# First attention: the transposes of the last chunk's heads stand before the values of the first half, not after them

## What is computed

```python
h = layer_norm(x, ln1_g, ln1_b)
qkv = (h @ w_qkv.T).reshape(B, S, 3, H, hd)      # 16 heads of 16
attn = sliding_window_attn(q, k, v, WINDOW, scale)   # chunks of 128, keys of this and the last chunk
x = x + attn @ w_o.T
```

## Time and profile before

| what | us |
|---|---|
| three runs | 1789.31, 1791.54, 1791.67 |
| median of the runs | 1791.54 |
| span of the profiled execution | 1791.1 |
| PE busy in the span | 1731.2 (97%) |
| first attention, s = 1 to 30 | about 29 to 354 us of the span |

### The profile page before, as it was taken

One profiled execution on the slowest core, in us unless ns is written; L12 is line 12 of the kernel. 1 busy time (PEld: TensorE's weight loads), 2 busy tenths in 40 slices (PEclk: granted clock), 3 DMA queues, 4 the chain that ended last, 5 costly groups with the idle time before them and its releaser, 6 DMA issues.

```text
span 1791.1 us, 43798 instructions
## 1 busy us (share of the span) xinstructions
PE 1731.2 (97%) x15424; PEld 1496.0 (84%) x15424; DVE 1494.1 (83%) x3797; ACT 1197.5 (67%) x3088; POOL 1080.0 (60%) x1060
## 2 busy tenths in 40 slices
PE   6999999999999999999999999989999999999997
PEld 4778777789998888888887888878888888888886
DVE  6888988868878898888987678789898898967776
ACT  6999988854445787877876334358787877743332
POOL 3676556534434778778773455377878777634343
PEclk9999999999999999999999999999999999999999
DMA  3111211032322111111112434331111111131221
GB/s 107 38 37 38 67 44 31 26 107 75 108 63 99 48 41 54 44 52 51 44 43 71 147 105 126 100 103 41 52 44 55 41 54 47 31 102 56 82 82 36
DMA packets 139812, 116.03 MB, mean 65 GB/s; under 512 B 10584, under 2 KB 138848, under 8 KB 138848
## 3 DMA queue, kind: packets, MB, share of 16 engines
q1 hardware_dynamic: 139616, 113.53, 20.5%
HBM read 75.74 MB, written 37.75 MB: 63 GB/s over the span
## 4 chain that ended last, share of the span: by engine, by line
PE 84%; DVE 9%; ACT 3%; issue 3%; POOL 0%; DMA 0%; SPq 0%; DVEq 0%; POOLq 0%; ACTq 0%
PE psum L567 17%; PE psum L569 17%; PE psum L568 17%; PE psum L906 6%; PE psum L874 5%; PE psum L887 5%; PE psum L682 3%; PE psum L664 3%; PE psum L848 3%; ACT a_probs L1718 2%; PE psum L920 2%; PE psum L617 1%; DVE a_neg_max L1211 1%; DVE psum L1209 1%; PE psum L654 1%
## 5 line engine op out<-in xcount | busy, mean ns | idle before, releaser
L1837 ACT ACTIVATE b_probs<-masked,neg_max 128x256 f32<-128x256 f32 (+1 forms) x512 | 250.6, 494 | 124.3 <-DVE neg_max L1343 124.3
L1343 DVE CUSTOM_DVE_ANT_0 masked<-psum,mask 128x256 f32<-128x256 f32 (+1 forms) x512 | 177.3, 412 | 75.9 <-PE psum L874 75.9
L567 PE MATMUL psum<-wa_hi,b_h_hi 128*128 128x512 f32 (+1 forms) x576 | 233.8, 406 | 6.9 <-DVE wa_lo L1138 3.9
L568 PE MATMUL psum<-wa_lo,b_h_hi 128*128 128x512 f32 (+1 forms) x576 | 214.0, 372 | 0.0
L569 PE MATMUL psum<-wa_hi,b_h_lo 128*128 128x512 f32 (+1 forms) x576 | 214.0, 372 | 0.0
L567 PE MATMUL psum<-g_h_hi,wm_hi 128*128 128x512 f32 (+1 forms) x480 | 190.5, 397 | 2.7 <-POOL g_h_lo L2121 1.6
L2070 POOL TENSOR_TENSOR g_in<-g_in,minus_half 128x16 f32<-128x16 f32 x64 | 188.2, 2940 | 4.5 <-DVE g_in L1295 4.5
L568 PE MATMUL psum<-g_h_lo,wm_hi 128*128 128x512 f32 (+1 forms) x480 | 189.3, 394 | 0.0
L569 PE MATMUL psum<-g_h_hi,wm_lo 128*128 128x512 f32 (+1 forms) x480 | 189.2, 394 | 0.0
L1458 POOL TENSOR_TENSOR g_in<-g_z,g_in 128x512 f32<-128x512 f32 x62 | 79.8, 1287 | 143.4 <-DVE g_in L1289 138.2
L567 PE MATMUL psum<-wm_hi,u_hi 128*128 128x256 f32 x576 | 164.3, 285 | 0.1
(11 more groups left out here) (169 smaller groups left out, 5644.0 us busy)
## 6 DMA issues: line engine op xcount, KB each, us to landing
x_mid<-y_out SPq DMA_DIRECT2D x96, 128.0 KB, 1.7
rope_in<-in_rope SPq DMA_DIRECT2D x64, 128.0 KB, 2.2
x_res<-x_state SPq DMA_DIRECT2D x64, 128.0 KB, 2.2
g_in<-x_mid SPq DMA_DIRECT2D x32, 256.0 KB, 3.8
g_old<-x_state SPq DMA_DIRECT2D x16, 512.0 KB, 4.0
out_x<-g_fin SPq DMA_DIRECT2D x15, 512.0 KB, 2.9
w_raw<-in_w_mlp_b SPq DMA_DIRECT2D x2, 2154.0 KB, 8.8
x_in<-in_x SPq DMA_DIRECT2D x32, 128.0 KB, 2.2
```

The source lines that it names most:

```text
L567: nc.tensor.matmul(out, a_hi, b_hi, start=first, stop=False)
L568: nc.tensor.matmul(out, a_hi, b_lo, start=False, stop=False)
L1343: ins = nc.vector.tensor_tensor_reduce(out[:, at], src[:, at], (mask if now else mask0)[:, at], -1.0, BIG, ALU.add, ALU.min, neg_max[:, r, ...
L1837: ins = nc.scalar.activation(out, src, ACT.Exp, bias=neg_max[:, r, k:k + 1], scale=-1.0, accum_out=row_sum[:, n % 2, 4 * r + k:4 * r + k + 1])
```

## The change

In `pe_attention_a`, `transpose_heads(s - 1)` is issued before `values(s, 0)` instead of after it. The waits inside both functions are unchanged, and travel with them. Step 0 has no last chunk, and in step 31 the transposes are issued elsewhere, so steps 1 to 30 differ.

```diff
                 if a_chunk(s):
                     transpose_probs(4 * s + 2)
-                    values(s, 0)
                 if a_chunk(s - 1) and s < NCH - 1:
                     transpose_heads(s - 1)
+                if a_chunk(s):
+                    values(s, 0)
```

## The result

The changed kernel takes 1815.41 us (median of 4 runs, 1812.95 to 1817.37) against 1791.61 us before (median of 4, 1789.31 to 1791.92). The ratio is 1.0133, with a 95% interval of 1.0118 to 1.0147: 1.3% slower, 23.8 us by the medians. The forecast was 1814.5 us, the range 1808 to 1820.

What follows compares the result with a forecast made beforehand. The first attention was taken as a ring of hand-overs among nearly full PE, ACT and DVE, with hardly any reserve. 28 x 0.77 + 2 x 0.70 = 23.0 us on the median 1791.54 gave 1814.5 us, range 1808 to 1820.

Steps and rivals of the forecast that it cites:

- The new wait, 0.77 us a step: Heads' transposes, now first, wait for DVE's q copy (`qt_ready`): 0.72 us plus 0.05 hand-over in each regular step.
- The hand-over from DVE: Time from the end of DVE's q copy to PE's heads load: taken as 0.05 us, up to 0.20 for the range.
- Behind the wait, 1.60 us in either order: On PE, heads 0.59 plus values 1.01 us take the same total, so next scores start 0.77 us later.
- The ring argument: Scores, exponentials, q, L1195, heads, values, scores form a closed ring without slack; the period goes from 10.8 to about 11.6 us.
- the rival of absorption: PE's 0.72 us idle before the probability transposes swallows the new wait: 1793.0 us, chance 0.03; half absorbed near 1803, 0.05.
- The odd steps, 0.70 each: The step opening the second batch and the one at 342.29: differences of 0.65 us, so each costs 0.70 instead of 0.77.
- The sum, 23.0 us: Whole first attention stage: 28 x 0.77 + 2 x 0.70 us, all arriving at the kernel's end.
- the earlier division of the heads: DVE divides heads while PE works on values; gain costed at nothing, as scores leave masking only 0.02 us to gain.
- The faster rival: Division of the heads leaves the chain of waits, taking 0.71 us a step off: 1770.2 us, chance 0.02.
- The clock: Rival: new PE idles lower the granted clock; a quarter of each step low loses 28 us, 1842 us; chance 0.05.
- The weight loads: Heads' first load could be pulled across the wait, saving 0.1 us a step, near 1811.5 us; not used in the sum.
- The signs: Expected in the profile: L693 idle some 0.8 us, L1195 11.5 to 11.6 us apart, ACT's idle before copies up about 0.8.

Runs made afterwards that it cites:

- the run with the wait alone: Old order, with only a wait for `qt_ready` added in front of the first half's values in the same 30 steps, against the kernel before: 1813.87 us, ratio 1.0126.
- The kernel with the heads after three quarters: Heads' transposes issued before the last 8 of the values' 32 matmuls, against the kernel before: 1795.72 us, ratio 1.0026.
- two transposes less: Old order with two of the four heads' transposes left out in chunks 0 to 29, against the kernel before: 1791.44 us, ratio 1.0000.
- the half split: Heads' transposes issued in the middle of the values, 16 of 32 matmuls in front, against the kernel before: 1802.44 us, ratio 1.0061.
- the last kernel: New order with ACT rounding q before exponentials 4s+2 and DVE's `finish_q_t` moved up, against the kernel before: 1808.39 us, ratio 1.0094.

## Why the prediction was right

*The new wait, 0.77 us a step.* Measured: a period of 11.58 against 10.80, 0.78. The hand-over from DVE was taken at 0.05 from another place of the trace and is 0.07 here (224.07 to 224.14). (The prediction counted two more waits behind the released one at that place. For the first chunk the code has one, as for the heads, so the row fitted better than was said.) The idle time in front of the heads is 0.96 or 0.97 us in 29 of the 30 steps and 1.01 in the first. It ends 0.07 us behind the end of L1196 (0.12 in the first), and the run with the wait alone shows that it is the cause.

*Behind the wait, 1.60 us in either order.* 0.59 + 1.01 again.

*Nothing absorbs it.* The 0.72 us in front of the probability transposes are unchanged. The ring argument (every link hangs on the late scores) was right, and from it the rival of absorption falls.

*The odd steps, 0.70 each.* The step at 342.29 before was 342.29 to 353.17, 10.88 us, and is 363.04 to 374.62, 11.58 us: 0.70 as forecast. The one that opens the second batch went from 10.71 us (201.33 to 212.04) to 11.05 us (212.27 to 223.32), only 0.34. There the old order already paid for a part of the delay, in two places:

```profile
201.63 1.19 ACT L1718 ACTIVATE a_probs<-psum,a_neg_max 128x128 f32<-128x128 f32 x4
...
202.15 0.42 PEld L693 LDWEIGHTS psum<-ident,rope_in 128*128 128x128 f32 x4 [0.32 <-issue]
...
202.93 0.22 PEld L654 LDWEIGHTS psum<-k_t_high,q_t 32*128 32x128 f32 x4 [0.36 <-DVE k_t_low L1184]
```

With half of the values the cover was too short. The copy of q ended at 202.08 and the heads loaded 0.07 us later, after 0.32 us idle instead of 0.20: this is the wait of the new order, small, in the old one. The scores then came 0.11 us behind the end of the exponentials (202.82), after 0.36 idle instead of 0.17. From values to scores this step took 202.93 - 201.43 = 1.50 us, and from heads to scores it takes 214.25 - 213.09 = 1.16 in the changed kernel, 0.34 less. The prediction had both forms equally long, so this term was 0.36 us too large.

*The sum, 23.0 us.* The first scores of the last step start at 354.80 before and 377.04 after, 22.24 us later. The first copy of q came 0.89 us earlier, so the 30 steps cost 23.1 us. That this is so near 23.0 is in part luck: the hand-over was 0.02 us too small in 30 steps (0.6 us), and the odd step 0.36 us too large. The medians are 23.8 us apart, with an interval of about 21 to 26 us, and carry the 23.

The profiled span grew by less, 20.1 us. Behind the stage the old execution loses lead in two places above all, both times where its clock was low. The low stretch of the earlier trace rows is not there in the changed kernel's execution, and the first matmul of the MLP is late by only 387.82 - 366.36 = 21.5 us. From 1564 to 1580 us the clock was 0.89 before, and it was 1.00 from 1585 to 1601 us in the changed kernel. The last L2070 of POOL moved from 1560.3 to 1581.5 us, 21.2 later, and ACT's L1852 at 1582.26 to 1602.33, only 20.07 later. The kernel with the heads after three quarters, whose clock was 0.89 from 1564 to 1580 us too, keeps its distance: the same two stand at 1565.9 and 1587.85, 5.6 us later both times. So most of what the spans lack against the cost of the stage comes from where the low stretches of the two executions fell. The 0.4 us between the old span and the median compare two different executions. Where the time and the span of one execution are both known, the time is about 1.75 us above the span (1812.95 and 1811.2). The forecast does not suffer from it, as it is the median plus 23.0.

*A reading that was too simple.* The prediction said that PE waits for no engine at the next scores, because the gap is called "issue", and priced the earlier division of the heads at nothing because scores leave 0.02 us. The price was right, but the picture lacked a link. The exponentials 4s+3 ended at 213.53 in the step of the earlier trace rows, and the scores started 0.14 us later:

```profile
212.34 1.19 ACT L1718 ACTIVATE a_probs<-psum,a_neg_max 128x128 f32<-128x128 f32 x4
```

With two transposes less PE was ready sooner and nothing was won. Three paths met there within 0.1 us: PE's order (213.67), these exponentials (213.53 and a hand-over of 0.12, 213.65), and DVE behind the division (214.49 less the 0.80 from scores to masking, 213.69). Each of them looked free or bound depending on which view was read.

*The faster rival* read the chain of waits at its face. The division of the heads did leave the chain, and DVE now waits for the scores (33.2 us in the waits above). What took their place is the wait in front of the heads.

*The clock.* At 1.00 from 30 to 345 us with PE busy for 91% of the time. The rule of the Trainium skill (TensorE: Matmul & The Clock Gate, A second HAM failure mode: psum-queue depth-cycling) did not come into play: an idle time of 0.96 us in each 11.6 us did not move the granted clock in this kernel.

*The weight loads.* The loads of the heads began with the release at 224.14 and not during the 0.96 us of idle time before it. The rule of the Trainium skill (TensorE: Matmul & The Clock Gate, Part 2: What happens when you issue a matmul), that weight loads are pulled ahead of matmuls in flight, took nothing off this wait.

*The signs.* Those of being right came, but for one in part: ACT's wait before its copy of the heads' values (L1736) grew to 10.8 us in 19 times, 0.57 each, and not by about 0.8 in every step.

## What to carry to other kernels

When a block is moved past another on an in-order engine, look up what each of its waits is released by and when. The block that stood in front may be the cover of a wait that the views of a regular step do not show, because it was over before PE came to it. Its price is the release minus the time at which the engine would get there, and it is paid in full where the engine's own delay feeds the releaser again in the next round. Adding the wait alone to the old order is a cheap way to tell the wait's cost from the order's. An irregular step, here the first one of a batch with half of the values as cover, can show the hidden wait before anything is changed.

## What the runs showed of the hardware

In regular steps, where nothing else held them, PE's weight loads stood idle for 0.17 us between a group of transposes (128 x 128) and the values (128 x 32) or scores (32 x 128) behind it, and for 0.20 us behind the values, before transposes and before scores. They did so also where the next matmul waited for nothing (217.00 in the half split). Between two groups of transposes there was no such gap, even with three waits in front of the second (110.02 in the last kernel). In a chain that PE alone sets, one more such change cost 0.14 us a step (11.72 against 11.58), and where the new order needed one less, the way from the probability transposes to the scores was 0.16 us shorter (2.03 against 2.19). What about the change of shape asks for this time was not tried.
